# A cross-attention, attention and expert kernel: new order of its first loads, four warm-up matmuls fewer

## The reference, cut to what matters

```python
# 1: cross-attention with a sigmoid, over all 25088 rows of ctx
h  = layernorm(x)
qp = h   @ Wq.T + bq          # 256 x 128
kp = ctx @ Wk.T + bk          # 25088 x 128
vp = ctx @ Wv.T + bv          # 25088 x 512
x  = x + sigmoid(qp @ kp.T / sqrt(128)) @ vp
# 2: causal attention of the 256 rows, 16 heads, with a rotary part
x  = x + attention(layernorm(x))
# 3: the best of 8 experts for each row
x  = x + experts(layernorm(x))
```

## Time and profile before

| What | us |
|---|---|
| Median of 3 runs (577.66 to 578.02) | 577.82 |
| The profiled execution's own time | 577.66 |
| Its span, from the first to the last instruction | 575.9 |
| PE busy, of the span | 569.3 (99%) |
| ACT busy, of the span | 401.6 (70%) |
| DVE busy, of the span | 457.6 (79%) |
| Warm-up matmuls (L265), 22 in all | 7.0 |

### The profile page before, as it was taken

The page is one execution under the profiler, slowest core; times in us unless marked ns, Lnnn a source line. Parts: engine busy times, 40 slices in busy tenths (PEclk is TensorE's granted clock), DMA queues, the critical chain, the costliest instruction groups (busy, mean ns, idle before and its releaser), DMA issues.

```text
span 575.9 us, 8082 instructions
## 1 busy us (share of the span) xinstructions
PE 569.3 (99%) x3010; PEld 477.5 (83%) x3010; DVE 457.6 (79%) x505; ACT 401.6 (70%) x540; POOL 1.7 (0%) x7
## 2 busy tenths in 40 slices
PE   9999999999999999999999999999999999999998
PEld 5888888888888888888888888888888887867887
DVE  5987878787878797879788978787878798888742
ACT  6776767676767787768777877776767684687321
POOL 1000000000000000000000000000000000000000
PEclk9999999999999999999999999999999999999999
DMA  8668787768677877787778777767686743000201
GB/s 330 220 198 234 246 238 238 233 213 245 211 223 250 261 247 226 249 261 250 233 242 260 251 223 253 220 219 227 211 283 228 226 139 124 22 1 2 74 0 38
DMA packets 33239, 115.90 MB, mean 201 GB/s; under 512 B 4080, under 2 KB 4784, under 8 KB 32944
## 3 DMA queue, kind: packets, MB, share of 16 engines
q1 hardware_dynamic: 32768, 115.05, 63.0%
q10 hardware_dynamic: 432, 0.33, 0.2%
HBM read 114.84 MB, written 0.52 MB: 200 GB/s over the span
## 4 chain that ended last, share of the span: by engine, by line
PE 95%; DVE 2%; ACT 2%; issue 0%; POOL 0%; POOLq 0%
PE ps L391 46%; PE ps L332 23%; PE ps L350 12%; PE ps L918 4%; PE ps L950 2%; PE ps L265 1%; PE ps L807 1%; PE ps L520 1%; ACT w L736 1%; PE ps L714 1%; PE ps L743 1%; PE ps L288 1%; PE ps L649 1%; PE ps L496 0%; DVE st L545 0%
## 5 line engine op out<-in xcount | busy, mean ns | idle before, releaser
L391 PE MATMUL ps<-nh,zh 128*128 128x512 f32 x388 | 142.7, 390 | 0.0
L391 PE MATMUL ps<-nh,zl 128*128 128x512 f32 x388 | 142.6, 389 | 0.1
L391 PE MATMUL ps<-nl,zh 128*128 128x512 f32 x388 | 142.5, 389 | 0.0
L365 DVE TENSOR_TENSOR zl<-zf,zh 128x1024 fp32r<-128x1024 f32 x49 | 60.1, 1226 | 81.7 <-ACT zh L364 81.7
L253 DVE TENSOR_TENSOR nl<-rawn,nh 128x1024 fp32r<-128x1024 f32 x96 | 113.7, 1218 | 0.8 <-issue 0.2
L233 DVE TENSOR_TENSOR tl<-rawt,th 128x1024 fp32r<-128x1024 f32 x96 | 112.8, 1215 | 0.2
L250 ACT ACTIVATE nh<-rawn 128x1024 fp32r<-128x1024 f32 x96 | 100.6, 1057 | 11.5 <-DMA rawn<-in_ctxn 10.8
L360 ACT ACTIVATE zf<-ps 128x512 f32<-128x512 f32 x98 | 58.5, 598 | 56.8 <-PE ps L350 50.9
L228 ACT ACTIVATE th<-rawt 128x1024 fp32r<-128x1024 f32 x96 | 96.2, 1052 | 0.0
L391 PEld LDWEIGHTS ps<-nh,zl 128*128 128x128 f32 x388 | 72.8, 188 | 15.5 <-DVE zl L365 0.5
L391 PEld LDWEIGHTS ps<-nl,zh 128*128 128x128 f32 x388 | 72.8, 188 | 15.1
(11 more groups left out here) (192 smaller groups left out, 620.4 us busy)
## 6 DMA issues: line engine op xcount, KB each, us to landing
rawn<-in_ctxn SPq DMA_DIRECT2D x97, 512.0 KB, 6.6
rawt<-in_ctxt SPq DMA_DIRECT2D x96, 512.0 KB, 5.0
h_s<-in_wg SPq DMA_DIRECT2D x4, 512.0 KB, 6.9
h_s<-in_wu SPq DMA_DIRECT2D x4, 512.0 KB, 7.3
wds<-in_wd SPq DMA_DIRECT2D x4, 512.0 KB, 4.0
raw<-in_ctxt SPq DMA_DIRECT2D x2, 512.0 KB, 8.4
h_s<-in_wvt SPq DMA_DIRECT2D x2, 512.0 KB, 7.3
wq_s<-in_wq SPq DMA_DIRECT2D x1, 1024.0 KB, 9.9
```

The lines of the kernel that those rows point to most:

```text
L365: ZL[b] = put("vector", lambda e: e.tensor_tensor(zl[b % 2][:], zf[:], zh[b % 2][:], ALU.subtract), [ZH[b]] + av, "zl")
L391: m = put("tensor", lambda e, z=z, n=n, i=i, j=j, r=r: e.matmul(bank(4 + r), z[:, j * T + r * P:j * T + r * P + P], n, start=(b == 0 and i ...
```

## The change

Three things are moved, and one number is changed:

- `wk_s` is issued by SP, third in its queue behind the two halves of `x`, instead of by ACT as its first instruction.
- The memset of `sq` and the dummy square root (`SQ0`, `WARM`) are appended ahead of ACT's two remaining DMAs. ACT thus loads its table first, and issues identity and biases behind it.
- There are 18 warm-up matmuls instead of 22.

```diff
         DX = [dma("sync", x_s[:, r, :], xr[:, r, :], f"dx{r}") for r in range(2)]
-        DWK = dma("scalar", wk_s[:], wkt, "dwk")
+        DWK = dma("sync", wk_s[:], wkt, "dwk")
+        SQ0 = put("vector", lambda e: e.memset(sq[:], 1.0), (), "sq0")
+        WARM = [put("scalar", lambda e: e.activation(sq[0:1, 1:2], sq[0:1, 0:1], ACT.Sqrt), [SQ0], "lnw")]
         DID = dma("scalar", id_s[:], ident, "did")
         wq0 = zf
         DBK = dma("scalar", bqk_s[:], bqk, "dbk")
@@
         WZ = put("gpsimd", lambda e: e.memset(wz[:], 0.0), (), "wz")
-        for k in range(22):
+        for k in range(18):
             put("tensor", lambda e: e.matmul(bank(7), wz[:, 0:P], wz[:], start=True, stop=True), [WZ])
         Z0 = put("gpsimd", lambda e: e.memset(zacc[:], 0.0), (), "pz")
         ONE = put("gpsimd", lambda e: e.memset(one_s[:], 1.0), (), "pz")
-        SQ0 = put("vector", lambda e: e.memset(sq[:], 1.0), (), "sq0")
-        WARM = [put("scalar", lambda e: e.activation(sq[0:1, 1:2], sq[0:1, 0:1], ACT.Sqrt), [SQ0], "lnw")]
         WKH = put("scalar", lambda e: e.activation(wkh[:], wk_s[:], ACT.Copy), [DWK], "wkh")
```

## The result

The changed kernel takes 579.03 us (median of 11 runs, 578.33 to 580.62), the kernel before 577.82 in the same session; the ratio is 1.0021, with a 95% interval of 1.0014 to 1.0029. I had forecast 577.3 with a range up to 578.1. The change makes the kernel slower, by about 1.2 us. The profiled execution took 578.64 us, with a span of 576.8 against 575.9 before.

A forecast was written before the change was run, and what follows sets the result against it. PE, holding 95% of the last-ending chain, bounds the kernel, so starting it earlier is kept one for one. The start-up shift of -0.50 us from 577.66 gives 577.2, with 0.16 for the median 577.3; range 576.7 to 578.1.

The forecast's parts named there:

- x alone: First load: without the key weights beside it, x lands 0.55 us earlier, `bn_stats` at 3.88; bounds 0 and about 1.2.
- Key weights third: SP's queue: behind both halves of x, the key weights land at 5.30 us, so `wkh` ends on ACT at 5.93.
- The square root: ACT, behind `wkh`: starts at 5.93 us instead of 6.43, a shift of 0.50.
- Identity and biases: ACT's DMAs behind table load and dummy: identity issued at about 2.25 us, landing 6.55, needed 7.56; costed at nothing.
- Warm-up: PE's start: the four matmuls dropped are fast ones, 0.86 us, worth nothing alone but the most PE can gain.
- Transposes: PE's first real work: transposes start at 7.56 us, first keys at 8.74 instead of 9.24.
- One for one to the end: PE's list after the start: whatever lets PE begin its real work earlier is kept to the end.
- A: Ahead of PE: gain lost through x, key weights or second context half; gain 0 to 0.2, 577.7 us; chance 0.27.
- C: Identity's DMA: lands late behind SP's context packets and holds PE, 578.3 to 580.0 us; chance 0.08.
- B: PE's cap: x lands 0.9 us or more earlier, everything follows, gain 0.86, 577.0 us; chance 0.11.
- D: TensorE's clock: drops to 1.2 GHz in PE's new gap, costing up to 2.4 us, 580.1 us; chance 0.04.
- Taking turns: DMA engines alternate packet by packet between queues with work, so x and key weights shared half and half, 51 beside 50.

The follow-up runs named there:

- e6: The changed kernel, with the key weights on SP behind the two halves of rawt instead of ahead of them: 583.21 us, ratio 1.0094 to the kernel before.
- e8: The changed kernel, with the key weights issued by ACT, held behind the dummy square root, identity and biases ahead: 582.85 us, ratio 1.0087 to the kernel before.
- e2: The changed kernel with 22 warm-up matmuls again: 578.56 us, ratio 1.0016 to the kernel before.
- e5: The changed kernel, with the biases issued by ACT only behind `wkh`: 579.11 us, ratio 1.0020 to the kernel before.
- e7: The changed kernel plus a second copy of the key weights by ACT's first DMA, the copy on SP staying: 578.82 us, ratio 1.0018 to the kernel before.
- e10: The changed kernel plus, first on ACT, a load of 32 bytes of each row of the context's first block: 578.77 us, ratio 1.0023 to the kernel before.
- e9: The kernel before, with the identity ahead of the key weights on ACT and 18 warm-up matmuls: 577.52 us, ratio 0.9991.
- e3: The kernel before, with only the key weights moved to SP: 578.88 us, ratio 1.0013.
- e14: The changed kernel, with rawt of block 0 loaded in four quarters, so 2 KB packets: 578.47 us, ratio 1.0009 to the kernel before.
- e1: The kernel before, with 18 warm-up matmuls instead of 22: 577.67 us, ratio 0.9996.
- e4: The kernel before, with ACT's table load and dummy ahead of identity and biases, key weights still first on ACT: 577.77 us, ratio 0.9999.
- e13: e9 plus 512 bytes of padding behind each 8 KB row of the transposed context: 577.34 us, ratio 0.9987 to the kernel before.
- e12: The changed kernel with 512 bytes of padding behind each 8 KB row of the transposed context: 578.08 us, ratio 1.0003 to the kernel before.

## Why the prediction was wrong

**The step that failed** is one sentence: "ahead of them stand the same bytes on the same engines, and their queue had work waiting for microseconds: I leave them at 6.95 and 8.4". The halves of rawt landed at about 8.7 and 10.0. I had asked whether SP's later issue matters (0.43 us, covered) and counted bytes, but took 400 GB/s for granted whatever the queues held. The 1.8 us went through a slack of 0.6 (from 6.95 to 7.56) for the first half and came out as 1.2 us against my forecast of PE's first keys: 9.95 for 8.74. I had allowed "at worst 0.4" for this term, and named no row for that bound. What makes the transfer slower is open, as said above; that it comes with the key weights' move is shown.

**Term by term.** x alone: right in kind, too small in size; I took 0.55 us and it was 0.90 (the first half took 2.8 us from issue to landing, for 3.7), since the pause behind the first packets went too: 205 GB/s moved from 2.0 to 2.5 us, and 8 in the kernel before. The upper bound of 1.2 had allowed for that. Key weights third: forecast 5.30, came at 5.54. The square root: 5.93, came at 6.08, and as forecast it was `wkh` that held it. Identity and biases: the premise was wrong, since ACT's DMAs did not wait for its table load here; issued at 0.90 instead of my 2.25, and no drain or landing mattered. Warm-up: the upper level came only at 6.78 us in this execution, so the four that went were not all fast ones, and the warm-up still ended at about the time of h_s. Transposes: 7.56, came at 7.69. One for one to the end: right.

**The rivals.** A named the late second context half, but as a loss of the gain only, with a floor at zero. C, a transfer late enough to hold PE, was the right mechanism on the wrong transfer: the identity landed at 3.7 us. B's condition came true, x 0.90 us earlier, but not what it forecast from it: `wkh` held the root at 6.08, 0.35 earlier, and its own objection, that the context would have to come sooner, was the point. D did not decide the median: in the profiled execution the matmuls behind the wait of 1.06 us keep their spacing. But the clock did fall after the stands of over 4 us in e6 and e8. And two of the changed kernel's 11 runs, 580.57 and 580.62 us, had a mean granted clock of 0.997 like the profiled runs of e6 and e8; so had one each of e2, e5 and e7 and two of e10, all with the key weights on SP, and none of the kernel before. So D's price, some 1.6 us, seems to be paid in some runs with the longer wait; none of these was profiled, so where the clock fell is not shown. No rival said that the change could make the DMA engines themselves slower, so the range ended 0.9 us too low.

**Taking turns.** That x and the key weights shared the engines half and half is borne out: when ACT's first DMA was again one of 256 KB beside x (e7), `bn_stats` went back to 4.52 us. e8 shows that beside other transfers the same 256 KB can take 7.2 us instead of 3.9.

## What to carry to other kernels

A transfer that moves to another queue changes more than the order of bytes: when a start-up chain hangs on a later transfer of the same queue, put the landing of that one, and not only of the one moved, into the sum with both ends, and a bound that includes half the usual rate. Look at the DMA rate in short stretches of the first microseconds, before and after, not at the mean. Here a swap of two DMAs on ACT's queue with four warm-up matmuls fewer (e9) gave 0.34 us in the trace, of the 0.50 that were forecast, with an interval of the time that just takes in 1. The two kernels that let the key weights wait longer (e6, e8) were the slowest of all, by about 5 us, because the square root stands behind `wkh` on ACT.

## What the runs showed of the hardware that I had not expected

- Sixteen DMA engines with work waiting moved 128 to 200 GB/s for 2 us in seven kernels with the key weights in SP's queue (the changed one and e2, e3, e5, e6, e10, e14), where they moved 321 to 370 in the three with them first in ACT's (the kernel before, e1, e4), with single packets of up to 2.2 us against 0.16 (0.08 for the 2 KB packets of e14). The others lay between, at 226 to 311, but for 405 in e13. Each figure is from one execution.
- ACT issued DMAs while its table load was running (at 0.90 us in a load from 0.73 to 2.01).
- The warm-up's matmuls rose to the upper level at 5.55 us in the kernel before and at 6.78 us in the changed one, from the same start at 1.31. In e4 it was 6.71, and there the 22 matmuls held the transposes till 8.44.
- 512 bytes of padding per 8 KB row were worth about 0.9 us to the changed kernel (e12), though the rate from 4.5 to 6.5 us rose only from 176 to 226 GB/s.
